# A recurrent layer with a top-2 mixture of experts on one core: expert work in pairs of 64-row halves on an unrolled timetable, against tiles of 128 rows in a loop

## The reference, cut to what matters

```python
# x (2, 1024, 256), h0 (2, 256), Wx, Wh (256, 256), 8 experts, inner size 1024, top 2
xW = einsum('ntd,dh->nth', x, Wx) + b
next_h = tanh(xw_t + prev_h @ Wh)                 # 1024 steps in a row, 2 sequences
...
logits = h_flat @ gate_w.T
top_v, top_i = top_k(logits, 2);  probs = softmax(top_v)
hidden = silu(h_flat @ wge.T) * (h_flat @ wue.T)  # each expert e
out    = sum over e of combine[e] * (hidden @ wde.T)
return x + out
```

## Time and profile before

| what | us |
|---|---|
| three runs, median | 1154.24 |
| lowest and highest of them | 1153.63, 1226.7 |
| the profiled execution's own span | 1152.2 |
| span of blocks 0 to 3 (12 to 282) | 270 |
| span of blocks 4 to 15 (282 to 1011) | 729 |
| after the last step (1011 to the end) | 141 |

### The profile page before, as it was taken

How to read it: one execution, slowest core, us unless ns; L and a number is a source line. 1 busy time by engine, 2 the same in 40 slices (tenths; PEclk the granted TensorE clock), 3 DMA queues, 4 the chain that set the end, 5 groups by cost and what they waited for, 6 DMA issues and landing times.

```text
span 1152.2 us, 42964 instructions
## 1 busy us (share of the span) xinstructions
PE 1115.8 (97%) x16126; PEld 759.0 (66%) x16127; DVE 454.5 (39%) x2369; ACT 453.3 (39%) x2730; POOL 92.7 (8%) x87
## 2 busy tenths in 40 slices
PE   9999999999999899999999899989999999999887
PEld 7666666666777676765777667766767767655554
DVE  3555556421444233432444333433243323452332
ACT  3455555422444333433444333433343324433332
POOL 0000000000101000100110100101010101011112
PEclk6555555555999857955999867985585757999999
DMA  4444444600010100000010101010100000311111
GB/s 115 129 122 137 134 133 134 205 11 16 17 21 17 23 12 16 22 12 18 17 26 17 28 7 21 17 23 16 21 17 11 17 6 19 95 34 23 25 26 23
DMA packets 36353, 51.36 MB, mean 45 GB/s; under 512 B 4497, under 2 KB 22802, under 8 KB 36114
## 3 DMA queue, kind: packets, MB, share of 16 engines
q1 hardware_dynamic: 29282, 39.37, 12.2%
q0 software_dynamic: 6864, 9.18, 4.9%
HBM read 34.90 MB, written 15.73 MB: 44 GB/s over the span
## 4 chain that ended last, share of the span: by engine, by line
PE 89%; DMA 5%; issue 3%; DVE 1%; ACT 1%; SPq 0%; POOLq 0%; ACTq 0%; DVEq 0%
PE bank L434 24%; PE bank L470 18%; PE bank L402 16%; PE bank L475 11%; PE bank L426 9%; DMA out<-y_sb,place_now 3%; PE bank L350 3%; PE bank L416 3%; PE bank L348 3%; DMA xrow<-expert_rows 2%; PE bank L391 1%; PE bank L514 1%; PE bank L378 0%; ACT y_sb L614 0%; SPq L239 0%
## 5 line engine op out<-in xcount | busy, mean ns | idle before, releaser
L470 PEld LDWEIGHTS bank<-hi,wh_hi 128*128 128x128 f16 x4096 | 267.7, 111 | 243.9 <-ACT hi L634 158.9
L634 ACT ACTIVATE hi<-bank 128x4 f16<-128x4 f32 x1024 | 179.4, 175 | 600.0 <-PE bank L475 598.9
L883 DVE TENSOR_TENSOR lo<-bank,hi 128x4 f16<-128x4 f32 x1024 | 166.9, 163 | 564.1 <-ACT bank L635 559.3
L434 PE MATMUL bank<-wh_hi 128*128 128x512 f16 (+3 forms) x970 | 348.9, 450 | 0.0
L470 PE MATMUL bank<-hi,wh_hi 128*128 128x2 f16 x4096 | 273.7, 171 | 13.4 <-issue 13.4
L475 PE MATMUL bank<-lo,wh_hi 128*128 128x2 f16 x4096 | 252.3, 165 | 0.0
L470 PE MATMUL bank<-hi,wh_lo 128*128 128x2 f16 x4096 | 247.5, 164 | 0.0
L402 PE MATMUL bank<-w_hi,x_T 128*128 x592 | 219.4, 428 | 4.5 <-issue 3.0
L470 PEld LDWEIGHTS bank<-hi,wh_lo 128*128 128x128 f16 x4096 | 181.9, 100 | 0.0
L475 PEld LDWEIGHTS bank<-lo,wh_hi 128*128 128x128 f16 x4096 | 179.9, 100 | 0.1
L635 ACT ACTIVATE bank<-bank 128x4 f32<-128x4 f32 x1024 | 173.3, 169 | 0.0
(11 more groups left out here) (120 smaller groups left out, 826.5 us busy)
## 6 DMA issues: line engine op xcount, KB each, us to landing
arena<-w_all SPq DMA_DIRECT2D x96, 256.0 KB, 2.7
xrow<-expert_rows SPq DMA_DIRECT2D x37, 132.0 KB, 2.1
expert_rows<-pad SPq DMA_DIRECT2D x32, 132.0 KB, 3.7
xt<-xT SPq DMA_DIRECT2D x16, 128.0 KB, 2.6
out<-y_sb,place_now POOLq DMA_INDIRECT x37, 3.8
expert_rows<-rows,slot POOLq DMA_INDIRECT x32, 2.6
arena<-wh_in SPq DMA_DIRECT2D x1, 256.0 KB
wx_sb<-wx_in SPq DMA_DIRECT2D x1, 256.0 KB
```

The costliest lines, as they stand in the source:

```text
L434: pe.matmul(bank[3][:, 0:min(n, 4) * P], wh_hi[:, 0, 0:P], wh_hi_cols[:, 0:min(n, 4) * P], start=True, stop=True, skip_group_check=True)
L470: pe.matmul(preact(i, tt)[:, B * m:B * m + B], w[:, k, m * P:(m + 1) * P], hi[:, pi, k, B * pt:B * pt + B], start=False, stop=False, skip_ ...
L634: act.activation(hi[:, i, :, B * tt:B * tt + B], src, ACT.Tanh, scale=1 / SCALE).then_inc(s_hi, 1)
L883: v.tensor_tensor(lo[:, i, :, B * tt:B * tt + B], h32[:, 4 * (tt % 2):4 * (tt % 2) + 4].rearrange("p (c b) -> p c b", c=2), hi[:, i, :, B ...
```

## The change

- **hi from the high products alone.** A step's eight products with `hi` are issued first (`hi_products(n + 1)`), and ScalarE's `hi_of(n + 1)` waits for these alone (`s_zh`). The four products with `lo` of step n follow, then `h32` of step n, then `lo`. `lo` so holds what `hi` left out, and hi + lo is the same sum. The x part and the sums take three PSUM banks in turn (step n in bank n mod 3), and the bias is put in by VectorE as a seed.
- **x part in f16.** `xw_mm` makes 36 matmuls a block of 42 or 44 columns from f16 pairs, one a step, in place of 12 in f32.
- **Halves of 64 rows.** Expert work comes in pairs: 64 rows of expert 2j and 64 rows of expert 2j + 1, j going round. The weights are now the stationary operand (128x128) and the 64 rows the moving one: 96 matmuls of 64 columns for gate and up of a half, 48 for down, 288 for a pair. The hidden values come out turned, so the f32 transposes of it are gone; the result yT is turned back with two (`turn_y`). The slice that a pair takes is given by counts (`make_slice`), the experts of a step are fixed when the program is written.
- **Timetable.** From step 208 on a pair takes 24 steps (`PERIOD`), 34 pairs up to step 1024, 10 to 14 of the 64-column matmuls in each step. All 1024 steps are written out; there is no loop over blocks. The filler brings each step to 14 units of 64 columns (24 units in steps 208 to 213); before step 208 there is none.
- **Scatters.** The rows of a block leave in four indirect DMAs of 64 rows at fixed steps; each half of a result is added with one of 64 rows, which waits until the one before has landed.
- **Tail.** After the last step two fixed pairs follow, then a list of pairs, four loops on PE (one for each two experts), each with at least one round.

The tables and filler, cut:

```diff
-DOWN_AT = (20, 21, 22, 23, 25, 26, 27, 28)
-FIRST = 4
...
+START, PERIOD, HALF_T = 208, 24, 12
+R = 64
+UNITS, FIRST_UNITS, FIRST_STEPS = 14, 24, 6
```

The step on the tensor engine:

```diff
-                pe.wait_ge(s_hi, n + 1)
-                for w in (wh_hi, wh_lo):
...
+                if n + 1 < T:
+                    hi_products(n + 1)
+                else:
+                    pe.wait_ge(s_hi, T + 1)
                 pe.wait_ge(s_lo, n + 1)
                 for m in range(2):
                     for k in range(2):
...
                 mm.then_inc(s_pre, 1)
-                if not tiles:
-                    keep_warm(6)
...
+                units = 0
+                if p >= 0:
+                    units += tile(p, o)
...
+                if p >= 0:
+                    keep_warm(free_cols(o), (FIRST_UNITS if n < START + FIRST_STEPS else UNITS) - units)
```

The step on ScalarE, and gate and up:

```diff
+                if n + 1 < T:
+                    hi_of(n + 1)
                 act.wait_ge(s_pre, n + 1)
-                src = preact(i, tt).rearrange("p (c b) -> p c b", c=2)
-                act.activation(hi[:, i, :, B * tt:B * tt + B], src, ACT.Tanh, scale=1 / SCALE).then_inc(s_hi, 1)
...
-                    mm = pe.matmul(dst[:], x_T[:, xpart, :], rhs, start=(n == 0), stop=(n == 3 * KC - 1),
-                                   skip_group_check=True)
...
+                    mm = pe.matmul(dst[:, c * R:(c + 1) * R], w[:, e, k * 2 * INNER + up * INNER + c * P:k * 2 * INNER + up * INNER + (c + 1) * P],
+                                   xs[:, xpart, half * R:(half + 1) * R], start=(n % (3 * KC) == 0),
+                                   stop=(n % (3 * KC) == 3 * KC - 1), skip_group_check=True)
```

The adds and the tail:

```diff
+                pool.wait_ge(s_acc, 32)
+                pool.wait_ge(s_y, weighed)
+                pool.wait_ge(s_scat, added)
...
+            for j in range(J):
+                with pe.Fori(to[j - 1] if j else DYN, to[j]) as p:
+                    whole_pair(p, j)
```

More of the change, by code:

```diff
@@ L136, in build @@
         pad = sb("pad", [P, ROWP], F32)
[L139 to L146, removed]
@@ L225, in build, with preact, fixed, expert @@
         block = ctx.enter_context(nc.Block())
[L227 to L243, removed]
+        def preact(n):
+            blk, t = divmod(n, STEPS)
+            c = blk % 2 * P + t // 3 * 2 * B
+            return xw[n % 3][:, c:c + 2 * B]
+        def fixed(v):
+            return isinstance(v, int)
+        def expert(p, half):
+            return 2 * (p % (E // 2)) + half
+        LISTED, ENDS = 11, 8
+        def end_of(eng, j):
+            return eng.value_load(ends[0:1, j:j + 1], min_val=1 + j, max_val=W) + DYN
+        def end_of_all(eng):
+            eng.wait_ge(s_ls, ENDS)
+            return end_of(eng, J - 1)
         def split_of(blk, tt):
-            n = blk * STEPS + tt - 4 if isinstance(blk, int) else -1
+            n = blk * STEPS + tt - 4
             return n if 0 <= n < 2 * NCH else None
@@ L501, in step @@
-                if ahead and tt == TURN_X_AT[0]:
-                    if not tiles:
-                        pe.wait_ge(s_up, UP * (blk - UP_FROM) + 1)
-                    turn_x(2 * (blk + 1 - FIRST))
-            def pair(pr):
-                for i in range(2):
-                    for tt in range(STEPS):
-                        step(pr * 2 + i, i, tt, **modes(pr, i))
-            pe.wait_ge(s_c, 3)
-            for _ in range(56):
-                pe.matmul(bank[3][:, 0:P], all1[:], all1[:], start=True, stop=True, skip_group_check=True)
@@ L539, in all_turn @@
[L539 to L549 removed]
+            hi_products(0)
+            for blk in range(NBLK):
+                for tt in range(STEPS):
+                    step(blk, blk % 2, tt)
@@ L563, in _ @@
[L563 to L576 removed]
+            logits(1, g)
@@ L767, in update @@
[L767 to L782 removed]
+                    v.wait_ge(s_rows, g * 4 + 4)
@@ L899, in step @@
-                if tiles:
-                    tile(blk, 0, tt - TILE_AT[0])
-                    tile(blk, 1, tt - TILE_AT[1])
-                    if tt == TAKE_AT[1]:
-                        take(2 * (blk - FIRST) + 1)
-                if ahead and tt == TAKE_AT[0]:
-                    take(2 * (blk + 1 - FIRST))
-                if split_of(blk, tt) is not None:
-                    split(split_of(blk, tt))
-            def pair(pr):
-                for i in range(2):
-                    for tt in range(STEPS):
-                        step(pr * 2 + i, i, tt, **modes(pr, i))
```

1334 lines of the change are left out of this document (746 added, 588 removed).

## The result

| | median us | lowest to highest | runs |
|---|---|---|---|
| before | 1181.43 | 1153.63 to 1226.7 | 5 |
| after | 884.87 | 882.14 to 1047.95 | 5 |

The ratio of the two is 0.768, with a 95% interval of 0.763 to 0.773: 23% faster. It leaves out the runs that a lower clock lengthened (1047.95 us after, the three of 1181 us and more before), so it is not the ratio of the two medians in the table. The forecast was 858 us with a range of 830 to 955.

What follows compares the result with a forecast made beforehand. PE bounds low-clock steps, the recurrence chain high-clock ones. Start 13.5, 208 chain steps 150.8, stall 3, dense steps 5, 816 steps 599.8, tail 83.5: 855.6 span, 858 us with what lies around it; range 830 to 955.

Steps and rivals of the forecast that it cites:

- The chain: Recurrence loop through lo: 0.71 us a step at either clock, from 0.78; 208 steps of chain alone take 150.8 us.
- the 3 us of stall at the first pair: First pair, loaded behind the copy of x to `out` and turned 11 steps later: PE stalls 3 us.
- PE in a step: Timetable steps on PE: twelve small matmuls 0.30, twelve 64-column ones at 30 ns 0.36, filler 0.06; 0.72 us at high clock.
- rivals of 57 ns: Expert matmuls in timetable and tail: 64 columns cost what 128 do, 57 ns; 1175 us, chance 0.06.
- an open load: Short expert matmuls: weight load not hidden, PE at low clock in the timetable, 80 ns a pair; 1450 us, chance 0.03.
- For collisions of such extras I add 0.015: Extra work of ScalarE and VectorE in the steps: 0.015 us added to each, making 0.735 in the timetable.
- Left for after the last step are ... 7: Tail: pairs 34 and 35 and a list of 2, 1, 1 and 1; 7 pairs at 9.3 us, 65.1.
- The rounds of the loops on PE: Tail: four loops on PE, five rounds at 1 us each, 5 us in all.
- The sum: Whole span: 13.5 + 150.8 + 3 + 5 + 599.8 + 83.5 = 855.6 us, 857.6 with what lies around it.
- I take it as high throughout: PE's clock after its rise in steps 208 to 213: stays at 2.4 GHz, so 816 steps of 0.735 take 599.8 us.
- the rival that I gave 0.13 in its two forms: Clock falls and stays low: halfway 145 us more, 1003, chance 0.09; from the start about 1147, chance 0.04.
- The chain keeps its length: Recurrence: a late tanh for hi pushes h32 on ScalarE; steps of 0.78, 51 us more, 909; chance 0.08.

Runs made afterwards that it cites:

- the first experiment: Changed kernel with the tanh for hi again waiting for all twelve products, right ahead of the one for h32: 916.06 us.
- the second experiment: Changed kernel with 14 units of filler instead of 24 in steps 208 to 213: 883.23, 899.5, 912.58 and 1142.86 us.

## Why the prediction was right, and where it was off

- **The chain.** Right in mechanism. The forecast of 0.71 against 0.78 is what the first experiment undoes, step by step: most places have 0.72 without the edit and 0.78 with it. Without expert work the median step is 0.733, not 0.71 (the loop of the earlier trace rows closes less tightly: the h32 tanh starts 0.31 behind the four products in some steps), and a few steps wait for weights, 2.3 us in all. 208 steps take 155.1 us, forecast 150.8. So the weights' stream is hidden but for 2 us here; two other profiles of the same kernel have waits for weights of 4.9 and 5.2 us and take 157.9 and 157.8 for these steps. The start is 10.2, not 13.5, and the 3 us of stall at the first pair did not come.
- **PE in a step.** Right: 29 ns for a short matmul (forecast 30), and at the low clock three take 0.16 us, 53 ns each, in these rows of the changed kernel's PE:

```profile
165.24 0.30 PE L492 MATMUL bank<-x_T,w_hi 128*128 128x64 f16 x2
...
165.40 0.30 PE L492 MATMUL bank<-x_T,w_hi 128*128 128x64 f16 x2
```

  The load of weights is hidden behind 64 columns as behind 128; the rivals of 57 ns (1175 us) and of an open load (1450) are refuted. But PE's 0.72 is not what sets the regular step, as the sum had it: with 12 units, where by the same sum PE needs 0.66, that step is the same. It is the chain's. The Trainium skill's 81 ns for a pair of load and matmul at 128 columns ("TensorE: Matmul & The Clock Gate", "Back-to-back issue gap") does not hold here: such pairs take 57 ns in the earlier trace rows, and those of 64 columns 29.
- **"For collisions of such extras I add 0.015".** This is the step that failed. The regular pattern is 0.729, below the 0.735 that the whole was to cost: extras of ScalarE and VectorE collide hardly at all. What is missing is 0.035 a step for PE's waits for its own program, which I had only named as something that would make the forecast wrong. Over 809 steps that is some 27 us; the regular pattern gives 5 back, and 22 of the 28 us by which the span is over are left. I had both numbers for it, 52 instructions in 0.73 us against 30 in 0.78, and gave it no price and no rival.
- **"Left for after the last step are ... 7".** The second failure: 8 pairs are left. I took block 14's counts as known when pair 34 is chosen, and they come two steps later. One pair is 9.3 us, by forecast and by measurement. The rounds of the loops on PE cost less than the 5 us set: in the profile only one waits for its issue, 2.2 us. The tail is 93.3 us, forecast 83.5.
- **The sum.** 883.5 span against 855.6: start -3.3, first 208 steps +4.3, dense steps and the stall at the first pair -4.5 (7.9 us measured, 12.4 forecast), the 809 distances of steps behind them +22.3 (616.96 against 594.62) less 0.7 for a step counted twice, tail +9.8. Together +27.9.
- **The clock.** That it rises in the dense steps is right, and the second experiment shows that they do it. "I take it as high throughout" holds, by their times, for 11 of 15 runs of the unchanged kernel. In four it fell (916, 1028, 1042 and 1048 us): the rival that I gave 0.13 in its two forms. Its price was about right: a fall from 409 to 955 us cost 163 us, and the forecast for half of the timetable was 145.
- **The chain keeps its length.** Refuted, and measured: 916 us, where the rival said 909.

## What to carry to other kernels

When a step shrinks, price the instructions in it as well as the columns: here 26 matmuls in 0.72 us were more than PE was given at every moment, 20 were not, and 26 in 0.78 us were not. Filler counts too: without it (0.7 matmuls and two units less in a step) more than half of what the stalls cost went. A chain and an engine balanced to 0.01 us leave no slack to take up such stalls, and 17 to 30 of the 61 us that the shorter chain promised were lost. Count the work left at the end from when each count is taken, to the step; one pair in the tail was a third of the error. And put two versions on the same chip before a difference of 1.5% is explained.

## What the runs showed of the hardware that I had not expected

- PE stops for 0.3 to 1 us without waiting for any engine, 22 to 39 times in 620 us, when 26 pairs of load and matmul stand in 0.72 us; 36 of 37 over 0.45 us, in three profiles, end 2.2 to 3.0 us after a 16 KB packet of instructions began to move. The sum differs between chips for the same kernel, 17.2 and 24.7 us.
- The granted clock is no function of the program. The same kernel held 2.4 GHz through the whole timetable, 640 us, or lost it at 409 for 546 us; with 12 units of filler it fell at 494 and came back at 562; without the dense steps it rose at 294 us in one run and in another, by its mean clock, not before the tail. Both falls in the timetable came within 2.4 us of the longest irregular stall of their run (0.99 and 0.71 us), so the supply of the program may cost more than its stalls; of the kernels with fewer stalls (the old chain, fewer instructions) none of eight runs lost the clock in the timetable, as far as their times and mean clocks tell, though the second lost it in the tail. That is suggested, not shown.
- An indirect add of 64 rows lands in 3.0 to 3.2 us (once 4.8), one of 128 in 3.8: half of the rows save 0.6 us, and the two adds of a pair each pay the rest.
